# High-part products first in every projection, a new order of the filling and emptying rounds, column sums in pieces, and added transposes

## The reference

```python
ln_out = layernorm(hidden_states, ln1_s, ln1_b)
ctx = merge_heads(attention(split_heads(q), split_heads(k), split_heads(v), ltor_mask))
x = hidden_states + ctx @ w_ao + b_ao                      # A
x = x + attention(layernorm(x) @ w_q, encoder @ w_kv) @ w_co + b_co   # B
x = x + gelu(layernorm(x) @ w1 + b1) @ w2 + b2             # M
return x + tanh(gate) * attention(x @ Wq.T, layernorm(ctx) @ Wk.T, ...) @ Wo.T   # C
```

## Time and profile before

| | us |
|---|---|
| median of 3 runs | 915.01 |
| lowest and highest | 912.89, 917.56 |
| the profiled execution's own time | 918.7 |
| its span, first to last instruction | 916.9 |
| PE busy, DVE, ACT, POOL | 860.6, 653.2, 576.4, 556.7 |

### The profile page before, as it was taken

One profiled execution on the slowest core, in us unless ns is written; L12 is line 12 of the kernel. 1 busy time (PEld: TensorE's weight loads), 2 busy tenths in 40 slices (PEclk: granted clock), 3 DMA queues, 4 the chain that ended last, 5 costly groups with the idle time before them and its releaser, 6 DMA issues.

```text
span 916.9 us, 24416 instructions
## 1 busy us (share of the span) xinstructions
PE 860.6 (94%) x9808; PEld 817.8 (89%) x9808; DVE 653.2 (71%) x1474; ACT 576.4 (63%) x1083; POOL 556.7 (61%) x565
## 2 busy tenths in 40 slices
PE   6687899999999999999999999999999999998885
PEld 5577888999999999999999999999999999998884
DVE  5746567778787787778787777778777777767543
ACT  5443555858485775858485776848485775748352
POOL 1436392948567592948567593948577592937231
PEclk9577899999999999999999999999999999999997
DMA  9000000010101010010101011010101010010000
GB/s 292 2 24 19 25 19 13 3 43 13 43 14 44 14 28 28 1 44 13 43 13 44 12 30 28 2 43 14 43 12 44 13 31 15 2 44 1 26 12 13
DMA packets 34142, 26.75 MB, mean 29 GB/s; under 512 B 12784, under 2 KB 33392, under 8 KB 34032
## 3 DMA queue, kind: packets, MB, share of 16 engines
q1 hardware_dynamic: 34032, 25.20, 9.3%
HBM read 20.99 MB, written 4.19 MB: 27 GB/s over the span
## 4 chain that ended last, share of the span: by engine, by line
PE 67%; DVE 19%; POOL 5%; issue 4%; ACT 3%; DMA 0%; DVEq 0%; SPq 0%; ACTq 0%; POOLq 0%
PE pj L456 21%; PE pj L475 13%; PE s_bank L539 11%; PE s_bank L525 8%; PE s_bank L514 6%; DVE vz_AC L1277 4%; PE pj L489 3%; PE pj L434 3%; DVE oT_AC_lo L1255 3%; DVE prob_AC L1285 3%; DVE stats L1325 2%; POOL prob_AC L1829 1%; PE pj L423 1%; DVE x L1309 1%; POOL prob_AC L1823 1%
## 5 line engine op out<-in xcount | busy, mean ns | idle before, releaser
L1809 POOL TENSOR_TENSOR rstd<-var_eps,half 128x2 f32<-128x2 f32 x64 | 46.7, 730 | 222.0 <-DVE var_eps L1336 222.0
L1829 POOL TENSOR_TENSOR prob_AC<-prob_AC,rmax_C 128x512 f32<-128x512 f32 x64 | 68.2, 1068 | 81.8 <-DVE rmax_C L1290 81.7
L943 ACT ACTIVATE prob_AC<-s_bank 128x512 f32<-128x512 f32 x128 | 73.7, 615 | 68.6 <-PE s_bank L525 68.3
L935 ACT ACTIVATE k<-pj,kbias,consts 128x256 f32<-128x256 f32 x192 | 92.6, 565 | 32.5 <-PE pj L456 30.0
L514 PE MATMUL s_bank<-k,q 64*128 64x128 f32 x1536 | 100.9, 281 | 8.5 <-ACT q L922 5.6
L514 PEld LDWEIGHTS s_bank<-k,q 64*128 64x128 f32 x1536 | 91.6, 190 | 15.4 <-ACT q L922 6.2
L1823 POOL TENSOR_TENSOR prob_B<-prob_B,maskB_off 128x512 f32<-128x512 f32 x64 | 81.5, 1285 | 14.0 <-DVE prob_B L1285 13.8
L1823 POOL TENSOR_TENSOR prob_AC<-prob_AC,maskA_off 128x512 f32<-128x512 f32 x64 | 81.0, 1275 | 13.5 <-DVE prob_AC L1285 13.5
L1836 POOL TENSOR_TENSOR h_lo<-g,h_hi 128x512 fp32r<-128x512 f32 x64 | 82.4, 1298 | 3.4 <-DVE h_hi L1794 3.4
L525 PE MATMUL s_bank<-consts,prob_AC 128*128 128x128 f32 x512 | 73.5, 282 | 11.1 <-POOL prob_AC L1829 8.1
L895 ACT ACTIVATE oT_AC_hi<-pj,bias 128x256 fp32r<-128x256 f32 x64 | 26.8, 471 | 87.8 <-PE pj L552 87.7
(11 more groups left out here) (207 smaller groups left out, 2937.1 us busy)
## 6 DMA issues: line engine op xcount, KB each, us to landing
x_in<-in_x SPq DMA_DIRECT2D x16, 256.0 KB, 2.7
ctx_b<-in_ctx_features SPq DMA_DIRECT2D x16, 256.0 KB, 3.0
ctx_c<-in_ctx SPq DMA_DIRECT2D x16, 256.0 KB, 3.1
out<-y SPq DMA_DIRECT2D x16, 256.0 KB, 2.2
maskB<-in_mask_Bx1xSxS_ff SPq DMA_DIRECT2D x32, 64.0 KB, 2.6
g<-in_w_M SPq DMA_DIRECT2D x2, 512.0 KB, 6.5
prob_AC<-in_w_A_qkv SPq DMA_DIRECT2D x3, 256.0 KB, 4.1
prob_B<-in_w_B_kv SPq DMA_DIRECT2D x2, 256.0 KB, 4.9
```

What stands on the lines that cost most here:

```text
L935: last = nc.scalar.activation(k2[:, m, :, s, :], k_all[:, m], ACT.Identity, bias=kbias[:, "ABC".index(a), s, m:m + 1], scale=parity[:, 2 + ...
L943: nc.scalar.activation(prob[a][:, r, :, :].rearrange("p n k -> p (n k)"), s_bank[r][:, :], ACT.Exp).then_inc(turned_in[a], 1)
L1809: nc.gpsimd.tensor_tensor(rstd[:, n, :], var_eps[:, n, :], half[:, :], ALU.pow).then_inc(ln_rstd[l], 1)
L1829: nc.gpsimd.tensor_tensor(p3, p3, rmax[a][:, r, :].unsqueeze(2).broadcast_to([P, BL * TILE, S]), ALU.subtract).then_inc(shifted[a], 1)
```

## The change

In every projection the eight products with the activations' high part come first, behind a wait for `hi_done` (for the MLP's output `h_hi_done`), and the four products with the low part follow behind a wait for the low part. The first matmul of the bank alone carries `start`. Twenty groups a round so have one more wait, in their middle.

The lists of `fill1`, `fill2`, `fill3`, `drain1`, `drain2` and `drain3` are put in another order on PE, ACT, DVE and POOL, and some calls cross a round: PE does B.V of unit 0 at the end of `fill1`, ACT's list of `fill3` stands at the end of `fill2`, and its lists of `drain2` and `drain3` at the end of `drain1` and `drain2`. `steady` is not touched. `carry_shifts` can be given in pieces: A in three, M in four (three of them in `fill1`, the last at the start of `fill2`), C in two. Low and high parts of the weights are spread otherwise over `fill0` to `fill2`.

New is `keep_busy`: four transposes of the identity, 128x128, into the bank of the PE group that follows, whose result nobody reads. It stands 33 times in PE's list: 6 in `fill0`, 13 in `fill1`, 3 in `fill2`, 1 in `fill3`, 1 in `drain1`, 2 in `drain2`, 7 in `drain3`. DVE's and POOL's `fill1` end with `moments` and `rstds` of stage B of the next round, and POOL's `rstds("A")` stands behind the last `shift`.

The diff, cut to its core:

```diff
+BUSY = 4
 
...
-    return [(name, i) for i in range(U + TAIL) for name in orders.get(phase(i), ())]
+    return [(name.rstrip("+"), i + name.count("+")) for i in range(U + TAIL) for name in orders.get(phase(i), ())]
...
 
-            def carry_shifts(l, i):
+            def carry_shifts(l, i, part=0, parts=1):
 
                 name = f"P.c{l}"
-                bank = claim(name, i)
+                bank = claim(name, i) if part == 0 else pj[pj_bank(name, i)]
                 at = SHIFT_AT[l]
+                columns = []
                 for use in SHIFTED[l]:
                     n = PIECE[use]
+                    for m in range((PIECES[n][7] - PIECES[n][6]) // P):
+                        columns.append((n, m, at))
+                        at += 1
+                size = len(columns) // parts
+                for n, m, at in columns[part * size:(part + 1) * size]:
                     pe.wait_ge(weights_in[n], 16)
                     w = PIECES[n][3]
                     shift = lnvec[:, LN[l], 1, :]
-                    for m in range((PIECES[n][7] - PIECES[n][6]) // P):
-                        for k in range(KC):
-                            last = nc.tensor.matmul(bank[:, at:at + 1], w[:, k, m * P:(m + 1) * P], shift[:, k:k + 1],
-                                                    start=(k == 0), stop=(k == KC - 1))
-                        at += 1
-                last.then_inc(pj_full[pj_bank(name, i)], 1)
+                    for k in range(KC):
+                        last = nc.tensor.matmul(bank[:, at:at + 1], w[:, k, m * P:(m + 1) * P], shift[:, k:k + 1],
+                                                start=(k == 0), stop=(k == KC - 1))
+                if part == parts - 1:
+                    last.then_inc(pj_full[pj_bank(name, i)], 1)
...
+            def keep_busy(following, i):
+
+                bank = claim(following, i)
+                for _ in range(BUSY):
+                    nc.tensor.transpose(bank[:, 0:P], ident[:, :], ident[:, :])
+
+            def wait_high(src, i):
+                pe.wait_ge(hi_done[src], unit(src[0], i) + 1)
+
+            def wait_low(src, i):
                 if src == "B.cT":
                     pe.wait_ge(ctx_low, unit("B", i) + 1)
                 else:
-                    pe.wait_ge(pj_free[pj_bank(src, j)], pj_use(src, j))
+                    pe.wait_ge(pj_free[pj_bank(src, i)], pj_use(src, i))
+
+            def feature_major(name, i):
+
+                src, w, col = FEATURE[name]
+                j = i - 1 if (name, src) == ("C.K", "M.cT") else i
+                hi, lo = OP[src]
+                wait_high(src, j)
                 first_weights(name, i)
                 if unit(name[0], i) == 0:
                     pe.wait_ge(bias_done, "ABMC".index(name[0]) + 1)
                 bank = claim(name, i)
                 for m in range(2):
-                    n = 0
+                    at = slice(col + m * P, col + (m + 1) * P)
                     for k in range(KC):
-                        for x, wt in parts(OP[src], w):
-                            last = nc.tensor.matmul(bank[:, m * TOK:(m + 1) * TOK],
-                                                    wt[:, k, col + m * P:col + (m + 1) * P], x[:, k, :],
-                                                    start=(n == 0), stop=(n == 3 * KC - 1))
-                            n += 1
+                        nc.tensor.matmul(bank[:, m * TOK:(m + 1) * TOK], w_hi[w][:, k, at], hi[:, k, :],
+                                         start=(m == 0 and k == 0), stop=False)
+                        nc.tensor.matmul(bank[:, m * TOK:(m + 1) * TOK], w_lo[w][:, k, at], hi[:, k, :],
+                                         start=False, stop=False)
...
                 bank = claim(name, i)
                 for t in range(T):
-                    n = 0
+                    at = slice(t * P, (t + 1) * P)
                     for k in range(KC):
-                        for x, wt in parts(OP[src], w):
-                            last = nc.tensor.matmul(bank[:, t * H:(t + 1) * H], x[:, k, t * P:(t + 1) * P],
...
+                        nc.tensor.matmul(bank[:, t * H:(t + 1) * H], hi[:, k, at], w_hi[w][:, k, col:col + H],
+                                         start=(t == 0 and k == 0), stop=False)
+                        nc.tensor.matmul(bank[:, t * H:(t + 1) * H], hi[:, k, at], w_lo[w][:, k, col:col + H],
+                                         start=False, stop=False)
+                wait_low(src, i)
+                for t in range(T):
+                    at = slice(t * P, (t + 1) * P)
+                    for k in range(KC):
...
+                pe.wait_ge(h_hi_done, GELU * u + GELU // 2 * (part + 1))
+                bank = pj[pj_bank(f"M.Y{t}", i)] if part else claim(f"M.Y{t}", i)
+                at = slice(t * P, (t + 1) * P)
+                inner = range(part * FF // P // 2, (part + 1) * FF // P // 2)
+                for k in inner:
+                    nc.tensor.matmul(bank[:, 0:H], h_hi[:, k, at], w_hi["M_2"][:, k, :], start=(k == 0), stop=False)
+                    nc.tensor.matmul(bank[:, 0:H], h_hi[:, k, at], w_lo["M_2"][:, k, :], start=False, stop=False)
                 pe.wait_ge(h_lo_done, GELU * u + GELU // 2 * (part + 1))
-                bank = pj[pj_bank(f"M.Y{t}", i)] if part else claim(f"M.Y{t}", i)
-                for k in range(part * FF // P // 2, (part + 1) * FF // P // 2):
-                    for n, (x, wt) in enumerate(((h_hi, w_hi["M_2"]), (h_lo, w_hi["M_2"]), (h_hi, w_lo["M_2"]))):
-                        last = nc.tensor.matmul(bank[:, 0:H], x[:, k, t * P:(t + 1) * P],
-                                                wt[:, k, :], start=(k == 0 and n == 0),
-                                                stop=(k == FF // P - 1 and n == 2))
+                for k in inner:
+                    last = nc.tensor.matmul(bank[:, 0:H], h_lo[:, k, at], w_hi["M_2"][:, k, :],
+                                            start=False, stop=(k == FF // P - 1))
                 if part:
...
             def fill0(i):
-                pass
+                keep_busy("P.cA", i + 1)
...
             def fill1(i):
-                carry_shifts("A", i)
+                carry_shifts("A", i, 0, 3)
                 pe.wait_ge(ln_done["A"], unit("A", i) + 1)
                 turn("A.zT", z["A"], i)
+                keep_busy("A.K", i)
+                keep_busy("A.K", i)
+                carry_shifts("A", 1, 1, 3)
+                carry_shifts("A", 1, 2, 3)
+                keep_busy("A.K", i)
                 feature_major("A.K", i)
                 feature_major("A.Q", i)
                 token_major("A.V", i)
+                carry_shifts("B", i, 0, 1)
                 scores("A", 0, i)
+                keep_busy("P.cM", i)
                 scores("A", 1, i)
+                keep_busy("P.cM", i)
+                keep_busy("P.cM", i)
+                carry_shifts("M", i, 0, 4)
+                keep_busy("A.OT", i)
+                keep_busy("A.OT", i)
+                carry_shifts("M", 1, 1, 4)
                 turn_probs("A", 0, i)
-                carry_shifts("B", i)
+                keep_busy("A.OT", i)
                 turn_probs("A", 1, i)
                 values("A", 0, i)
+                keep_busy("A.OT", i)
+                keep_busy("A.OT", i)
                 turn_probs("A", 2, i)
                 turn_probs("A", 3, i)
                 values("A", 1, i)
+                keep_busy("A.OT", i)
+                carry_shifts("M", 1, 2, 4)
                 turn_out("A", i)
+                keep_busy("A.AO", i)
                 token_major("A.AO", i)
+                token_major("B.V", i + 1)
 
             def fill2(i):
-                carry_shifts("M", i)
-                token_major("B.V", i)
+                carry_shifts("M", 1, 3, 4)
+                feature_major("B.K", i)
+                pe.wait_ge(ln_done["B"], unit("B", i) + 1)
+                turn("B.zT", z["B"], i)
                 pe.wait_ge(ln_done["A"], unit("A", i) + 1)
                 turn("A.zT", z["A"], i)
-                pe.wait_ge(ln_done["B"], unit("B", i) + 1)
-                turn("B.zT", z["B"], i)
...
                 values("A", 1, i)
                 token_major("B.AO", i)
                 turn_out("A", i)
+                carry_shifts("C", i, 0, 2)
+                keep_busy("A.AO", i)
                 token_major("A.AO", i)
...
+            def drain2(i):
+                pe.wait_ge(ln_done["M"], unit("M", i) + 1)
+                turn("M.zT", z["M"], i)
...
+                keep_busy("M.Y0", i)
+                keep_busy("M.Y0", i)
+                values("C", 0, i)
+                values("C", 1, i)
+                mlp_out(0, 0, i)
+                turn_out("C", i)
...
+            def drain3(i):
+                pe.wait_ge(tokens["M"], T * (unit("C", i) + 1))
+                turn("C.xT", x3, i)
+                feature_major("C.K", i)
+                feature_major("C.Q", i)
```

(59 more changed lines are left out.)

454 lines of the change are left out of this document (227 added, 227 removed).

## The result

| | before | after |
|---|---|---|
| median (range), runs | 915.72 us (912.89 to 917.56), 4 | 888.79 us (886.11 to 890.51), 4 |
| profiled execution, its span | 918.7, 916.9 us | 887.4, 885.6 us |

The ratio is 0.9706, 95% interval 0.9667 to 0.9745: faster by 26.9 us. The forecast was 877, with 865 to 884 as its band. One execution of the kernel before, timed later beside the experiments, was slow (1632.13 us) and is left out everywhere.

What follows compares the result with a forecast made beforehand. PE was taken to bound the 13 steady rounds, with idle and half-speed time in filling and emptying; 9.8 + 21 + 7.5 = 38.3 us off gave 877 us from the median of 915.0, range 866 to 896.

Steps and rivals of the forecast that it cites:

- the first: Filling and last round: keep_busy does not raise the clock, half speed stays; about 12 us lost, 889 us; chance 0.18.
- the third rival: Rounds 2 and 3: POOL's chain of offsets and shifts and shared k2 bind filling; 9 of 21 come, 889 us; chance 0.13.
- High part first, steady rounds: 13 steady rounds: PE's wait for the low part ahead of groups goes; 0.75 us a round, 9.8 us in all.
- Rounds 0 and 1: Start of filling, up to the turn of z_B: reordered lists, overlap and full speed bring about 10 us.
- 4.1 us by which PE was late for z_B: Round 1: M's column sums and B.V delayed z_B's turn; moving three pieces and B.V into gaps gives 4.1 us.
- 4.1 + 1.3 + 0.8 - 1.0 = 5.2: Round 1: PE's lateness 4.1, full-speed A.AO 1.3, A.zT's turn 0.8, less low parts ahead of tokens on DVE 1.0.
- 1.3 + 0.9 + 1.4 + 1.5 - 0.7 = 4.4: Rounds 0 and 1: rstds off POOL's chain, A.AO's overlap, full-speed transposes/values/turn, earlier scores, less a keep_busy and sums piece.
- Rounds 2 and 3: Filling: early B.K, rstds off the chain, clock and A.AO's overlap give 5 us, less idle and half speed 6 us.
- Emptying: Emptying rounds: 3 us from less idle in rounds 17 and 18, 4.5 in the last round; 7.5 us in all.
- The 3.6 for full speed in the last round: Last round: full speed for transposes, values, turn and C.AO gives 1.0 + 0.9 + 0.4 + 1.3 = 3.6 us.
- The second: Middle of each group, 20 a round: the added wait stops PE's stream; at 0.19 us each, 938 us; chance 0.03.
- The fourth: Filling and emptying: crossing lists add a wait for each removed, only the steady part counts; 905 us; chance 0.04.

Runs made afterwards that it cites:

- The two attempts to win the time back: Changed kernel with B.AO, M.H3 and half of M.Y1 moved in PE's steady list: 911.53 us; with POOL's rstds for A and ACT's z_A moved later: 890.42 us.
- the low wait ahead: Changed kernel with new lists and transposes kept, but the wait for the low part again ahead of each group: 903.55 us, ratio 0.9854.
- the second profiles: Both kernels run again unchanged: the changed kernel 886.71 us, ratio 0.9683; the kernel before 912.77 us in one execution.
- M.H3 ahead: Changed kernel with rstds off POOL's unbroken row and M.H3 ahead of the fourth transposes of C in steady rounds: 890.63 us, ratio 0.9704.
- the three runs with an edited filling: Changed kernel with four edits in rounds 1 and 2: 887.22 us; those plus both steady edits: 890.27; M's column sums in one piece: 893.45.

## Why the prediction was right, and by which steps it was not

The direction and the range, 866 to 896, held; the forecast did not. The sum, 38 us, was 11 too large on medians, and 888.8 lies outside the 865 to 884 that had a chance of 0.60. It lies on the 889 of the first and the third rival, and the range held it because its high end was drawn to hold them. (That end and the low one take 10 and 26 for the filling, where the text had given 8 and 30.) So the range was right in part by luck. The steady rounds were not luck: 50.8 to 51.0 us was said and 50.98 measured.

**High part first, steady rounds.** Taken 0.75 a round, measured 0.62, and 0.68 alone. The mechanism and the three places were right, and they gave more than was taken. Averaged over the 13 rounds, A.AO starts 0.12 us after the matmul before it instead of 0.58, C.AO 0.03 after the last transpose instead of 0.39, B.Q 0.12 instead of 0.33, and within A.AO and B.Q another 0.1 each is gone, where I had subtracted for the restart of the stream: 1.23 together. The step that failed is "ACT, DVE and POOL keep their lists there and have 150 us or more of slack over the 670.8; what is late next is PE's own work". POOL is busy for 450 of 663 us, but from the second shift of C to the last of A its instructions stand without a gap, 29.4 of the 51 us, and the end of that row is what PE now meets: the transposes of the probabilities take 0.60 longer a round (0.51 at A and C, 0.09 at B). With the low wait ahead again they are back at their old length to 0.02. An engine's slack has to be read between two events that PE waits for, not over the stretch. The two attempts to win the time back moved the wait to other places, so what POOL's row costs is read from the trace and not confirmed by a faster kernel.

**Rounds 0 and 1.** Taken 10, measured 6.5 (5.6 between the second profiles). The sum held one term twice: the turn of A.zT (0.8) is part of the 4.1 us by which PE was late for z_B. Behind the start of A.AO 4.1 + 1.3 + 0.8 - 1.0 = 5.2 were taken and 5.6 came, from 12.95 us to 7.32 up to the turn of z_B. The 4.1 came as predicted. The other 1.5 were DVE's and not the full speed of A.AO, whose first eight products still ran at half and which gained 0.35. DVE starts the moments 0.84 us after the tokens, where the low parts of a weight and of the context had stood between and made it 2.31 (first the kernel before, then the changed one):

```profile
45.17 0.68 DVE L1309 TENSOR_TENSOR x<-pj,xb_A 128x512 f32<-128x512 f32 x1
...
47.48 0.74 DVE L1325 BATCH_NORM_STATS2 stats<-x 128x6 f32<-128x256 f32 x2
```

```profile
43.84 0.69 DVE L1375 TENSOR_TENSOR x<-pj,xb_A 128x512 f32<-128x512 f32 x1
44.68 0.75 DVE L1391 BATCH_NORM_STATS2 stats<-x 128x6 f32<-128x256 f32 x2
```

Ahead of the start of A.AO 1.3 + 0.9 + 1.4 + 1.5 - 0.7 = 4.4 were taken, and this is where the prediction failed: A.AO starts at 41.20 instead of 42.12 (41.30 instead of 41.42), 0.9 and 0.1 earlier. The first scores, taken 1.5 earlier, did not come earlier at all (21.79 and 21.35 against 22.01 and 21.45). And in both profiles the clock was at half through the piece of sums, the turn and A.AO, despite the transposes around them. Where an execution happened to have full clock there (M.H3 ahead), A.AO began at 39.35 and z_B turned at 46.54.

**Rounds 2 and 3.** Taken 5 and 6, measured 3.8 and 6.2. Of the third rival one half is true here: the shared `k2` leaves PE a wait of 3.9 us in round 2, and filling it brought nothing.

**Emptying.** Taken 7.5, measured 6.8; but against the second profile of before only 911.0 - 814.5 - 92.7 = 3.8. The 3.6 for full speed in the last round were one execution's. Without any transposes the last round takes 23.3 instead of 23.0.

**The sum.** I took every half-speed item out of an execution at clock 0.966 and subtracted them from the median, though executions of that kernel have clocks of 0.963 to 0.977. The profiles differ by 31.3, the medians by 26.9; the profiled execution of before lay 3.0 above its median, that of after 1.4 below.

**The rivals.** The first (889) gave nearly the measured time by a cause that is wrong as stated. Its rule, from the Trainium skill's "TensorE: Matmul & The Clock Gate", part 4, is contradicted by the rise at 8.95 us behind transposes alone. But its half about the clock not following is true in part: the transposes are worth 2 to 5 us, not 12, and in both profiles the clock was at half between them around A.AO. The second is refuted by the added waits. The third (889) is right that POOL's row sets round 2, and the same row limits the steady rounds, where I had not looked for it; its price is not what happened, for 16.5 of the 21 us of the filling came and not 9, and the filling ended at 130.1 and not after 135. The fourth is refuted by the run with the low wait ahead.

What stays open: why the clock falls in the first 70 us while PE is busy, and whether an edit further down the list can change it ahead of its own place, as the three runs with an edited filling leave possible. No run shows what would hold it there.

## What to carry to other kernels

When a wait is removed from the bounding engine, look for the engine whose unbroken row of work ends just before that engine's next need; its mean busy share does not show it. A wait in the middle of an accumulation group cost nothing measurable when its semaphore was up (662.6 against 662.8 us with 64 more a round), so a group can be split where its operands come in two steps. Compare at least two profiles of the same kernel before pricing a clock effect, and move one instruction past another only after reading what the other engines' fixed lists expect at that place.

## What the runs showed of the hardware that was not expected

- Transposes of a constant raise TensorE from 1.2 to 2.4 GHz: full speed is first recorded at 6.7 to 9.1 us in ten profiles with 24 of them at the start, at 18.3 to 20.1 in four without.
- The same program gets different clocks in different executions: in the changed kernel half speed ran from 15.8 to 19.2 and from 36.3 to 43.1 us in one profile, from 14.4 to 17.8 and from 34.9 to 45.1 in the other, and its total spreads over 7 us.
- DVE's cast of 128x512 took 0.41 to 0.43 us alone or beside POOL's 128x2 instructions. Begun under one of POOL's additions or shifts of 128x512 it ended 0.28 us behind that instruction, in 59 of 62 cases of two profiles: 0.66 us when 0.38 of it was left, 1.33 when 1.05 was.
- 64 additional waits a round, each already satisfied, cost nothing: 13 rounds took 662.6 us with them and 662.8 without.
